# Attention and experts on one core: weights times V for four key tiles in a row, one maximum product behind each score tile

## The reference, cut to what matters

```python
xn = _layernorm(x)                       # x is 1 x 2048 x 128
q, k, v = xn @ Wq, xn @ Wk, xn @ Wv      # 16 heads of 64
attn = softmax(q k^T * 64 ** -0.5)       # 2048 x 2048 for each head
attention = (attn v) @ Wo + bo
e = argmax(xn @ router_w^T)              # one of 8 experts for each token
ffn = square(relu(xn @ expert_fc[e])) @ expert_proj[e]^T
out = x + attention + ffn
```

## Time and profile before

| What | Value |
|---|---|
| median of three runs | 1500.65 us (1494.28 to 1501.56) |
| span of the profiled execution, first to last instruction | 1494.8 us |
| mean granted PE clock, as a share of 2.4 GHz | 0.989 |
| PE busy | 1450.1 us (97%) |
| DVE busy | 1259.4 us (84%) |
| POOL busy | 794.5 us (53%) |
| ACT busy | 680.9 us (46%) |

### The profile page before, as it was taken

How to read it: one execution, slowest core, us unless ns; L and a number is a source line. 1 busy time by engine, 2 the same in 40 slices (tenths; PEclk the granted TensorE clock), 3 DMA queues, 4 the chain that set the end, 5 groups by cost and what they waited for, 6 DMA issues and landing times.

```text
span 1494.8 us, 23270 instructions
## 1 busy us (share of the span) xinstructions
PE 1450.1 (97%) x6444; PEld 844.8 (57%) x6444; DVE 1259.4 (84%) x1252; ACT 680.9 (46%) x1286; POOL 794.5 (53%) x607
## 2 busy tenths in 40 slices
PE   5889999999999999999999999999999999999998
PEld 3545655556655566555565556656556555555543
DVE  7788888888898888888889888898888888889965
ACT  4244444444444444444444444444444444444443
POOL 8285554555544555554555554555544554467555
PEclk9799999999999999999999999999999999999999
DMA  2333110331121311213112131122201220001000
GB/s 78 85 89 92 38 40 27 79 84 23 38 61 48 83 38 26 59 45 84 40 31 71 39 73 40 39 67 70 57 18 40 66 66 22 22 14 37 1 15 15
DMA packets 66100, 73.25 MB, mean 49 GB/s; under 512 B 8992, under 2 KB 39072, under 8 KB 65952
## 3 DMA queue, kind: packets, MB, share of 16 engines
q1 hardware_dynamic: 64928, 69.44, 18.9%
q0 software_dynamic: 1024, 2.10, 0.5%
HBM read 18.42 MB, written 5.24 MB: 16 GB/s over the span
## 4 chain that ended last, share of the span: by engine, by line
PE 86%; DVE 10%; issue 3%; POOL 1%; DMA 0%; ACT 0%; SPq 0%; POOLq 0%; DVEq 0%; ACTq 0%
PE OB L947 29%; PE SB L918 17%; PE SB L922 14%; PE MB L935 14%; DVE acc L655 3%; DVE mx L639 3%; DVE rd L760 2%; PE XB L993 2%; PE XB L975 2%; PE XB L984 1%; PE XB L902 1%; PE XB L909 1%; PE XB L954 1%; PE XB L956 1%; PE XB L955 1%
## 5 line engine op out<-in xcount | busy, mean ns | idle before, releaser
L400 POOL TENSOR_TENSOR acc<-acc,ex 128x512 f32<-128x512 f32 x448 | 600.3, 1340 | 549.5 <-ACT ex L497 548.5
L497 ACT ACTIVATE ex<-SB 128x512 f32<-128x512 f32 x1024 | 556.3, 595 | 651.1 <-PE SB L922 644.1
L639 DVE TENSOR_REDUCE mx<-MB 128x1 f32<-128x1024 f32 x512 | 618.5, 1214 | 197.5 <-PE MB L935 194.8
L947 PE MATMUL OB<-ex,V 128*64 128x512 f32 x2048 | 497.6, 605 | 0.0
L655 DVE TENSOR_TENSOR acc<-acc,ex 128x512 f32<-128x512 f32 x448 | 469.6, 1048 | 12.3 <-ACT ex L497 11.7
L918 PE MATMUL SB<-Q,K 128*128 128x512 f32 x1024 | 440.6, 430 | 4.3 <-issue 3.9
L922 PE MATMUL SB<-Q,K 128*128 128x512 f32 x1024 | 403.8, 394 | 0.0
L918 PEld LDWEIGHTS SB<-Q,K 128*128 128x128 f32 x1024 | 192.6, 188 | 254.4 <-issue 208.4
L935 PE MATMUL MB<-K,Q 128*128 128x512 f32 x1024 | 285.2, 399 | 7.3 <-DVE mx L639 5.7
L947 PEld LDWEIGHTS OB<-ex,V 128*64 128x64 f32 x2048 | 126.8, 136 | 230.2 <-issue 199.3
L935 PEld LDWEIGHTS MB<-K,Q 128*128 128x128 f32 x1024 | 192.6, 190 | 57.7 <-DVE mx L639 12.0
(11 more groups left out here) (121 smaller groups left out, 585.8 us busy)
## 6 DMA issues: line engine op xcount, KB each, us to landing
Q<-qhi SPq DMA_DIRECT2D x124, 128.0 KB, 2.3
K<-khi SPq DMA_DIRECT2D x112, 128.0 KB, 2.3
Q<-qlo SPq DMA_DIRECT2D x64, 128.0 KB, 2.3
K<-klo SPq DMA_DIRECT2D x56, 128.0 KB, 2.4
w<-fc SPq DMA_DIRECT2D x24, 256.0 KB, 2.7
w<-projT SPq DMA_DIRECT2D x24, 256.0 KB, 3.1
sorted_x<-res SPq DMA_DIRECT2D x1, 1536.0 KB, 7.2
tok<-sorted_x SPq DMA_DIRECT2D x24, 64.0 KB, 1.7
```

Of the source, the lines that this page charges most:

```text
L400: pool.tensor_tensor(a[:, :], src[:, :], EX[1][kt % RING][:, :], ALU.add).then_inc(g_a, 1)
L497: act.activation(EX[h][kt % RING][:, :], SB[h][:, :], ACT.Exp).then_inc(a_e, 1)
L639: dve.tensor_reduce(mx[:, m % 2, u:u + 1], MB[i % 2][:, :], AX.X, ALU.max).then_inc(v_m, 1)
L947: mm = pe.matmul(OB[own[h], :], V[(n // JB) % 2][:, k, own[h]], EX[h][k % RING][:, :], start=(k == 0), stop=(k == NT - 1))
```

## The change

Four things change. times_v is called at every fourth key tile (kt = 4, 8, 12 and 0 of the next block) for four tiles in a row, the order of the two heads alternating from tile to tile. The ring of exponentials grows from four slots to six for each head: tiles 0 to 14 go round in slots 0 to 4, and tile 15 has slot 5 to itself. The units no longer come in twos at odd tiles, but one behind the scores of each tile. And to make room in SBUF, several buffers share memory: the routing tables lie in the experts' weight buffers w1 and w2 and in up, hid is up (squared in place), and on is osb (normalised in place). The last block still calls times_v for one tile at a time.

```diff
-RING = 4
+SLOTS = 6
+BATCH = 4
...
-        EX = [[sb(f"ex{h}{k}", [P, QB]) for k in range(RING)] for h in range(2)]
+        EX = [[sb(f"ex{h}{k}", [P, QB]) for k in range(SLOTS)] for h in range(2)]
...
+        hid = up
...
+        pick, mask, total, cum = (w1[:, k * E * NT:(k + 1) * E * NT].rearrange("p (e t) -> p e t", e=E) for k in range(4))
+        place, gate = (w2_flat[:, k * E * NT:(k + 1) * E * NT].rearrange("p (e t) -> p e t", e=E) for k in range(2))
...
+        on = osb
...
+        def ex_slot(kt):
+
+            return SLOTS - 1 if kt == NT - 1 else kt % (SLOTS - 1)
+
+        def slot_before(n, kt):
+
+            if kt == NT - 1:
+                return n - 1, kt
+            return (n, kt - SLOTS + 1) if kt >= SLOTS - 1 else (n - 1, kt + NT - SLOTS)
...
-                        old = (n, kt - RING) if kt >= RING else (n - 1, kt - RING + NT)
-                        if n.i is not None or n.off > 0 or kt >= RING:
+                        old = slot_before(n, kt)
+                        if old[0].i is not None or old[0].off >= 0:
                             wait(act, t_pv, old[0].times(NT, old[1] + 1))
                             wait(act, (v_a, g_a)[h], added(*old))
...
                     for k in range(kt, kt + tiles):
-                        for h in (0, 1) if k == kt else (1, 0):
-                            mm = pe.matmul(OB[own[h], :], V[(n // JB) % 2][:, k, own[h]], EX[h][k % RING][:, :],
+                        for h in (0, 1) if (k - kt) % 2 == 0 else (1, 0):
+                            mm = pe.matmul(OB[own[h], :], V[(n // JB) % 2][:, k, own[h]], EX[h][ex_slot(k)][:, :],
...
-                        for m, u in (unit(n, kt - 1), unit(n, kt)) if kt % 2 else ():
-                            if before(m, NB):
-                                max_unit(m, u)
+                        m, u = unit(n, kt)
+                        if before(m, NB):
+                            max_unit(m, u)
...
-                        elif kt % 2 == 0:
+                        elif kt % BATCH == 0:
                             if kt:
-                                times_v(n, kt - 2, 2)
+                                times_v(n, kt - BATCH, BATCH)
                             elif not start:
-                                times_v(n - 1, NT - 2, 2)
+                                times_v(n - 1, NT - BATCH, BATCH)
```

More of the change, by code:

```diff
@@ L138, in layer @@
         rw = sb("rw", [P, E])
-        pick, mask, total, cum, place = (sb(n_, [P, E, NT]) for n_ in ("pick", "mask", "total", "cum", "place"))
         top, slot = sb("top", [P, NT]), sb("slot", [P, NT], U32)
         tiles_of, end, first_tile = (sb(n_, [P, E]) for n_ in ("tiles_of", "end", "first_tile"))
-        past, owner, owner_i = sb("past", [P, TILES, E]), sb("owner", [P, TILES]), sb("owner_i", [P, TILES], I32)
-        before_p, gate = sb("before_p", [P, P]), sb("gate", [P, E, NT])
+        owner, owner_i = sb("owner", [P, TILES]), sb("owner_i", [P, TILES], I32)
         falling, tokens_in, tile_no, one_e = (
@@ L148, in layer @@
         tok, tokT, w1, w2 = sb("tok", [P, D]), sb("tokT", [P, P]), sb("w1", [P, HD]), sb("w2", [P, NC, D])
-        up, hid, res = sb("up", [P, NC * P]), sb("hid", [P, NC * P]), sb("res", [P, D])
+        up, res = sb("up", [P, NC * P]), sb("res", [P, D])
+        hid = up
+        w2_flat = w2[:, :, :].rearrange("p c d -> p (c d)")
+        pick, mask, total, cum = (w1[:, k * E * NT:(k + 1) * E * NT].rearrange("p (e t) -> p e t", e=E) for k in range(4))
+        place, gate = (w2_flat[:, k * E * NT:(k + 1) * E * NT].rearrange("p (e t) -> p e t", e=E) for k in range(2))
+        before_p = w2_flat[:, 2 * E * NT:2 * E * NT + P]
+        past = up[:, 0:TILES * E].rearrange("p (r e) -> p r e", e=E)
         sorted_x = nc.dram_tensor("sorted_x", (TILES * P, D), F32, kind="Internal").ap()
         sorted_y = nc.dram_tensor("sorted_y", (TILES * P, D), F32, kind="Internal").ap()
-        osb, rd, on = sb("osb", [P, QB]), sb("rd", [P, QB]), sb("on", [P, QB])
+        osb, rd = sb("osb", [P, QB]), sb("rd", [P, QB])
+        on = osb
         mx, nm = sb("mx", [P, 2, UNITS]), sb("nm", [P, 2, UNITS // 2])
@@ L399, in add @@
                         src = a
-                    pool.tensor_tensor(a[:, :], src[:, :], EX[1][kt % RING][:, :], ALU.add).then_inc(g_a, 1)
+                    pool.tensor_tensor(a[:, :], src[:, :], EX[1][ex_slot(kt)][:, :], ALU.add).then_inc(g_a, 1)
                 def normalise(n):
@@ L492, in exps @@
                         wait(act, t_s, n.times(2 * NT, 2 * kt + h + 1))
-                        old = (n, kt - RING) if kt >= RING else (n - 1, kt - RING + NT)
-                        if n.i is not None or n.off > 0 or kt >= RING:
+                        old = slot_before(n, kt)
+                        if old[0].i is not None or old[0].off >= 0:
                             wait(act, t_pv, old[0].times(NT, old[1] + 1))
                             wait(act, (v_a, g_a)[h], added(*old))
-                        act.activation(EX[h][kt % RING][:, :], SB[h][:, :], ACT.Exp).then_inc(a_e, 1)
+                        act.activation(EX[h][ex_slot(kt)][:, :], SB[h][:, :], ACT.Exp).then_inc(a_e, 1)
                 def split_w(pair):
@@ L654, in add @@
                         src = a
-                    dve.tensor_tensor(a[:, :], src[:, :], EX[0][kt % RING][:, :], ALU.add).then_inc(v_a, 1)
+                    dve.tensor_tensor(a[:, :], src[:, :], EX[0][ex_slot(kt)][:, :], ALU.add).then_inc(v_a, 1)
                 def low_w(pair):
```

## The result

The changed kernel takes 1602.63 us in the median (1600.45 to 1605.42) against 1501.11 us before: a ratio of 1.0689 with a 95% interval of 1.0666 to 1.0712. It is 101.5 us slower. The forecast was +64 us, slower by the mechanism named, and the time lies 2.6 us above its range.

The account below looks back on a forecast made before the run. PE's stream was taken as the bound. Per block -1.08 + 2.2 + 0.8 = +1.92 us, times 30 = +58, with block 0 +7 together +65, giving 1565 us; range 1525 to 1600.

Parts of the forecast that it names:

- the mechanism named: PE at unit 8, blocks 1 to 30, waits for the reduction behind the reciprocal: 2.0 to 2.7 us a block.
- What the batches save: V products on PE, blocks 1 to 30: three fewer half-width passages of 0.36 us, 1.08 us a block, 32 us.
- The wait at unit 8: PE reaches unit 8 after 3.43 us, released at 5.61 behind the denominators: 2.2 us in each of 30 blocks.
- The clock: Rival: PE's clock falls after the wait, 2.6 us once a block, 78 us more, 1643 us; chance 0.09.
- Small waits that V used to cover: PE at kt = 7, kt = 11 and scores waiting for exponentials: 0.8 us a block, between 0 and 1.2.
- Block 0: PE stops at unit 12 behind the ranking, POOL's addition for tile 9 comes later: 7 us, between 0 and 9.
- What costs nothing: Ring of exponentials and shared buffers: no cost; a late load of expert weights would come once, not each block.
- The rivals: Clock falls 0.09; passages win, 1469 us, 0.05; wait and saving cancel, 1500 us, 0.04; DVE behind in every group 0.04.
- DVE falls behind in every group: Rival: between batches DVE is slower than PE, 1.4 us at three more places a block, 1690 us; chance 0.04.

Follow-up runs that it names:

- the kernel with copies: The changed kernel with the 31 reciprocals of blocks 1 to 31 replaced by plain copies of the same tile: 1515.75 us, ratio 1.0113.
- the run with waits 0.6 us longer: The changed kernel with one more reduction of the denominators' tile, its result unused, ahead of each reciprocal: 1616.69 us, ratio 1.0791.

## Why the prediction was wrong in size, point by point

**What the batches save: right.** A batch of eight products took 3.58 us where 0.15 + 8 x 0.43 = 3.59 was forecast, and there are five passages a block. I have no run that weighs the 1.08 us by itself; it stands on these rows.

**The wait at unit 8: right.** Forecast 2.2 us in each of 30 blocks (66 us), measured 61.5 of idle, mean 2.05. The chain is the one given: reciprocal 1.13 us behind the denominators (1.08 forecast), 3.27 us to the reduction (3.26), unit 8 released 5.62 us behind the denominators (5.61). In the block shown PE could have been there after 3.63 us instead of 3.43, since the scores of tile 4 waited for the exponentials; those 0.2 us are covered by the wait. Not foreseen were the six blocks with 3 us, where the low part of the weights at tile 1 makes DVE later. The run with tile 4 in another order and the one with copies show that this wait, with its consequences, is most of the loss.

**The clock: the step that failed.** It stood among the rivals as all or nothing, 2.6 us in every block or none, with a chance of 0.09 and no share in the sum. It came in part. By the mean clocks 51 us of full speed were lost instead of 16, 35 us more, some 29 of them in the blocks behind block 0. Falls were seen behind 14 of the 30 waits, each costing some 1.6 us instead of 2.6, in blocks alike in all else, and at the two turns of the loop. The row at 1.13 us idle without a fall and the one at 3.88 with it had left this open, and the sum should have had a share of the 78 us in it. How large a share, no row of the kernel before could tell; half of it would have given 1604 us, but that is hindsight.

**Small waits that V used to cover: the second term that was too small.** Forecast 0.8 us a block, with 1.2 as the upper bound; the kernel with copies shows 1.5, which is 21 us more in 30 blocks. The places were right: from scores to scores 1.57 us in the median where 1.38 were needed. I had counted 0.11 us for each. What I missed is that a product that waits also starts worse: the next one follows 0.34 us behind it instead of 0.23 (746.93 to 747.27). So each place costs 0.19 instead of 0.11. Of the 0.7 us that were missing this explains about 0.4, at five places a block; where the rest comes from stays open.

**Block 0: right.** Forecast +7 us, with PE stopped at unit 12 behind the ranking and POOL late at the end. The two waits as they came:

```profile
83.28 1.22 PE L952 MATMUL MB<-K,Q 128*128 128x512 f32 x2 [6.48 <-DVE mx L656]
```

```profile
118.78 1.98 PE L1001 MATMUL XB<-acc,ones 128*64 128x512 f32 x4 [4.54 <-POOL acc L417]
```

6.48 us at unit 12 and 4.54 us for POOL instead of 3.88, both with products at half speed behind them; the first reciprocal is 7.9 us later.

**The sum again,** with what was measured: 30 x (-1.08 + 2.05 + 1.5) = +74, block 0 +8, the clock in the blocks behind it near 30, together about +112 against a span that grew by 108.8 us. The forecast had +65. Against it the clock brings near 30, the small waits 21, and the wait 4.5 less. With either of the first two as forecast the time would have stayed within the range; the clock is the larger.

**What costs nothing: right.** The slots and shared buffers measured 0.9992 [0.9977, 1.0008]. An expert's weights were not waited for in the changed kernel; in the run with the denominators together with V they were, once, for 3.47 us.

**The rivals.** That DVE falls behind in every group did not come: in the loop no unit but unit 8 waited 0.25 us or more. What remains open is why the clock falls behind one wait of 1.82 us and not behind the next; with waits of 2.40 to 2.58 us it fell behind fewer, so the length of this wait does not decide it alone.

## What to carry to other kernels

Work that is moved on the engine that bounds a kernel may save its own overhead and still lose, because it was the cover of another engine's longest instruction. Before batching, list for each long instruction elsewhere (here a reciprocal of 3.35 us) everything that waits for it, the bank that it holds as well as what stands behind it, and count the work that lies between; when the cover is gone, moving only the first waiter brings out the next. And where a wait of the matrix engine grows, put an expected share of a fall of its clock into the sum; here it was 14 falls behind 30 waits, at some 1.6 us each.

## What the runs showed of the hardware

The granted clock fell to its lower level (1.2 GHz) behind idles of 1.82 us in some blocks and not in others (11 of 23 at 1.80 to 1.98 us, three of six at 3 us), and in the run with waits 0.6 us longer the mean clock was higher (0.973 against 0.968), with five falls of 23 at 2.40 to 2.58 us and six of six at 3.6. A score product that had to wait was followed by the next after 0.34 us instead of 0.23. At the two turns of the loop PE stands idle for 1.85 and 2.09 us in the kernel before, without a fall, and for 3.10 and 2.90 in the changed one, where the clock fell both times. It did not always: in the run with only tile 4 in another order it fell at the turn of 2.73 us and stayed up at the one of 3.08. The reciprocal of 128 x 512 took 3.35 us on DVE, the copy of the same tile 0.69.
